# Attention on one core: the value product in two bursts a head, and two heads turned at once

## The chip, the cores and the metric

The kernel runs on one core of one Trainium2 chip. The metric is device time in microseconds (us). The program computes a small transformer in one launch: attention, a mixture of experts, a wavelet block with linear attention, and a second mixture of experts. The change touches the attention stage and a constant that it used.

## The reference

`x` has 4 sequences of 1024 tokens and 256 features; there are 16 heads of 16 features, so 64 (sequence, head) pairs. All is float32.

```python
Q, K, V = (proj(Wq, bq), proj(Wk, bk), proj(Wv, bv))
scale = 1.0 / jnp.sqrt(jnp.float32(hd))
scores = jnp.einsum('bhqd,bhkd->bhqk', Q, K) * scale
attn = jax.nn.softmax(scores, axis=-1)
out = jnp.einsum('bhqk,bhkd->bhqd', attn, V)
```

## The kernel before, in words

`stage_attention` works through the 64 heads, four to a loop iteration (`SLOTS`), first and last iteration written out (`peeled_ends`). Each engine has its own program and they meet at semaphores. For head n, with the 1024 keys in eight tiles `kt` of 128:

- TensorE (PE) makes transposed scores of a key tile, 128 keys by 1024 queries, as two products of 512 columns into `p_s[kt % 2]` (L507). ScalarE (ACT) takes the exponential into `pt` in SBUF (L541).
- Two heads ahead, PE makes the scores a second time, queries on partitions, in units of 128 by 512 (`max_unit`, L432), and VectorE (DVE) reduces each to a row maximum (L555). There are two units, `max0` and `max1`, for every `kt`. POOL negates the maxima and splits them into bf16 parts, PE turns them into rows (`rows_unit`, L440), DVE copies those (L569), and they enter the scores as two extra rows of the stack.
- These units go through `ring`, three PSUM banks. `claim(at)` makes PE wait until `ring_used` has reached `at - 2`, that is, until DVE has used unit `at - 3` and all before it.
- The value product `pv` (L454) multiplies `pt` by the padded values (16 features, a column of ones for the sum, zeros up to 32). Its result has only 32 rows, so four products run beside one another in the four column groups of the array: group `j = 2*qh + kh` takes query half `qh` and the even or odd key tile of the pair `2*i`, `2*i + 1`. One head has four such bursts of four calls, i = 0, 1, 2 after the scores of `kt` 3, 5, 7 and i = 3 after `kt` 1 of the next head. Each fp32 call shows as two records in the trace.
- ACT copies the accumulated `p_o`, 128 by 512, into `o_sb` (L530) after the exponential of `kt` 1 of the next head. `fold_unit` (L464) then multiplies each 128-column block by `c.fold`, which turns it (tokens onto partitions) and adds the halves for even and odd key tiles. The result goes into a ring bank, and DVE normalises from it (L577 reciprocal, L579 multiply).

The order of units in a head is written out in `units`: `max0`, scores, `rows` at `kt` 2, `max1`, burst, `fold` at `kt` 4. All engines derive the ring numbers from that list.

Of the kernel before, what the change touches and what calls it, by code (L numbers as in the profile page):

```python
# [8 lines left out]
ALU = mybir.AluOpType  # L9
# [89 lines left out]
def stage_constants(nc, mem, c):  # L99
# [3 lines left out]
    c.fold = mem.sb("fold", [P, 2 * 32])  # L103
    zeroed, made = mem.sem("consts_zeroed"), mem.sem("consts_made")
    with nc.Block() as block:
        @block.gpsimd
        def _(pool):
            nc.gpsimd.memset(c.ident[:, :], 0.0).then_inc(zeroed, 1)
            nc.gpsimd.memset(c.identb[:, :], 0.0).then_inc(zeroed, 1)
            nc.gpsimd.memset(c.fold[:, :], 0.0).then_inc(zeroed, 1)  # L110

            pool.wait_ge(zeroed, 3)
# [3 lines left out]

            fold = c.fold[:, :].rearrange("p (q r) -> p q r", q=2)
# [147 lines left out]
def stage_attention(nc, a, c, w1, w1_loaded):  # L265
# [8 lines left out]
    with ExitStack() as stack:  # L274
# [5 lines left out]
        o_sb = mem.sb("o_transposed", [P, HALF])  # L280
# [5 lines left out]
        rec = mem.sb("o_reciprocal", [P, 2, 4])  # L286
# [18 lines left out]
        FOLD_AT, ROWS_AT = 4, 2  # L305

        def units(first, last, u):

            for kt in range(KT):
# [6 lines left out]
                if kt == FOLD_AT and not (first and u == 0):  # L316
                    yield kt, "fold"
# [10 lines left out]
        PER_GROUP = SLOTS * (2 * KT + 2)  # L328
        assert PER_GROUP % RING == 0 and GROUPS == w1.shape[1]

        def count_before(g, first, last, u):

            inside = sum(len(list(units(first, last, w))) for w in range(u))
            if first:
                return PROLOGUE + inside
            return g * PER_GROUP + (PROLOGUE - 1 + inside)

        def bank(g, first, last, u, j):
            base = PROLOGUE if first else PROLOGUE - 1
# [7 lines left out]
        with nc.Block() as block:  # L347
# [40 lines left out]
            def _(pool):  # L388
# [36 lines left out]
            def _(pe):  # L425
# [18 lines left out]
                def pv(n, u, i):  # L444

                    pe.wait_ge(exp_done, n * KT + 2 * i + 2)
# [32 lines left out]
                def body(g, first, last):  # L479
                    for u in range(SLOTS):  # L480
# [5 lines left out]
                        def emit(kt, kinds):  # L486
                            for j, (step, kind) in todo:
# [5 lines left out]
                                elif kind == "fold":  # L493
                                    fold_unit(n - 1, at, out)
# [24 lines left out]
                pv(NH - 1, SLOTS - 1, KT // 2 - 1)  # L519
                end = count_before(GROUPS - 1, False, True, SLOTS)  # L520
                fold_unit(NH - 1, end, bank(GROUPS - 1, False, True, SLOTS, 0))

            @block.scalar
            def _(act):
                def copy_o(n, units_before):

                    act.wait_ge(pv_done, (n + 1) * (KT // 2))

                    act.wait_ge(ring_ready, units_before)
                    nc.scalar.activation(o_sb[:, :], p_o[:, :], ACT.Copy).then_inc(o_copied, 1)  # L530

                def body(g, first, last):
                    for u in range(SLOTS):
                        n = g * SLOTS + u
                        for kt in range(KT):

                            act.wait_ge(scores_ready, n * KT + kt + 1)
                            if kt % 2 == 0:

                                wait_from(act, pv_done, (n - 1) * (KT // 2) + kt // 2 + 1)  # L540
                            nc.scalar.activation(pt[:, kt, :], p_s[kt % 2][:, :], ACT.Exp, scale=SCALE)\  # L541
                                .then_inc(exp_done, 1)
                            if kt == 1 and not (first and u == 0):
                                copy_o(n - 1, count_before(g, first, last, u))
# [1488 lines left out]
```

## Time and profile before

| | us |
|---|---|
| median of 3 runs | 2200.02 (2199.92 to 2202.66) |
| span of the profiled execution | 2200.1 |
| attention stage, first ring product to last multiply | 114.3 to 932.3 |
| of 225 to 900 us: PE / DVE / ACT / POOL busy | 675.0 / 592.0 / 462.7 / 49.1 |
| one reduction, 128x512 | 0.686 |
| one exponential, 128x1024 | 1.022 |
| copy of `p_o`, 128x512 | 0.597 |

The profiled execution's own time is the span, 0.1 us from the median. "Busy" is the union of the records of an engine. Matmul records overlap and their ends are modelled, so PE's work is better read from the distance between starts. A timeline row merges equal neighbours; "x3" are three instructions, and the duration is that of all of them. "PEld" rows are weight loads. "[0.35 <-PE ps_ring L432]" means that the engine had been idle for 0.35 us and that this product ended it.

### The profile page before, as it was taken

The numbers are of one execution on the slowest core, as the hardware profiler recorded it, in microseconds if no ns is written. First come the engines' busy times: TensorE is split into PE (matmuls) and PEld (weight loads), VectorE is DVE, ScalarE is ACT, GpSimd is POOL, SyncE is SP. The second block draws the span as 40 slices with busy tenths as digits, with TensorE's granted clock in tenths as the row PEclk, the third lists the DMA queues.
The fourth block names the chain that finished last, engine by engine and source line by source line (L and its number), as shares of the span: only waits on it lengthen the run. The fifth ranks groups of instructions, "written<-read, shape, count | busy, mean of one in ns | idle before, by whom it ended". The sixth has DMA issues, their size and how long they took to land. (4 is left out here: it accounts for less than half of the span.)

```text
span 2200.1 us, 36075 instructions
## 1 busy us (share of the span) xinstructions
PE 1873.4 (85%) x9396; PEld 1027.7 (47%) x9397; DVE 1405.8 (64%) x3053; ACT 890.4 (40%) x1235; POOL 420.3 (19%) x561
## 2 busy tenths in 40 slices
PE   7899999999999999985699999999994885057771
PEld 4423333333333333363467766666673565036550
DVE  4588888888888888552744444444444897936335
ACT  3336666666666666732022222222221520021330
POOL 2210000000000000030023333333331001102771
PEclk9979999999999999987799999999997998575995
DMA  4511111111111111056111111221212000061224
GB/s 141 182 43 40 42 45 45 46 39 42 42 38 46 39 42 45 28 180 242 64 29 31 32 33 30 33 33 30 33 31 81 1 1 6 19 224 48 47 39 153
DMA packets 98995, 130.04 MB, mean 59 GB/s; under 512 B 19392, under 2 KB 78080, under 8 KB 98304
## 3 DMA queue, kind: packets, MB, share of 16 engines
q1 hardware_dynamic: 66400, 85.79, 12.4%
q0 software_dynamic: 21504, 23.72, 6.5%
q10 hardware_dynamic: 11040, 19.92, 2.6%
q8 instruction: 24, 0.39, 0.1%
q14 instruction: 27, 0.22, 0.0%
HBM read 94.93 MB, written 48.23 MB: 65 GB/s over the span
## 5 line engine op out<-in xcount | busy, mean ns | idle before, releaser
L555 DVE TENSOR_REDUCE unit_max<-ps_ring 128x1 f32<-128x512 f32 x1024 | 655.6, 686 | 85.1 <-PE ps_ring L432 74.8
L541 ACT ACTIVATE w<-ps_scores 128x1024 f32<-128x1024 f32 x512 | 509.8, 1022 | 268.2 <-PE ps_scores L507 256.4
L432 PE MATMUL ps_ring<-k_stack,q_stack 96*128 96x512 bf16 x1024 | 372.2, 392 | 9.8 <-POOL v_padded L395 9.2
L1272 PE MATMUL m_ps_y<-w,m_ht 128*128 (+1 forms) x1312 | 305.3, 382 | 32.3 <-DVE m_ht L1358 32.3
L507 PE MATMUL ps_scores<-q_stack,k_stack 98*128 98x512 bf16 x1024 | 306.6, 381 | 0.1
L1250 PE MATMUL m_ps_h<-w,m_xt 128*128 (+1 forms) x736 | 305.4, 554 | 1.2 <-ACT m_xt L1305 1.0
L454 PE MATMUL ps_o<-w,v_padded 128*32 128x512 f32 x2048 | 273.3, 606 | 0.6 <-ACT w L541 0.6
L1272 PEld LDWEIGHTS m_ps_y<-w,m_ht 128*128 128x128 f32 x1312 | 241.0, 190 | 68.5 <-DVE m_y L1366 33.4
L432 PEld LDWEIGHTS ps_ring<-k_stack,q_stack 96*128 96x128 bf16 x1024 | 102.2, 100 | 317.7 <-DVE unit_max L555 232.3
L1186 POOL DMA_INDIRECT sums<-m_y,m_is x112 | 177.8, 1588 | 266.7 <-ACT m_y L1298 244.7
L1365 DVE COPY m_is<-scatter 128x1 int32 (+1 forms) x112 | 17.3, 154 | 293.5 <-PE m_ps_y L1272 222.1
L1315 ACT ACTIVATE m_h<-m_h 128x512 f32<-128x512 f32 (+1 forms) x184 | 107.3, 583 | 238.2 <-DVE m_h L1348 237.1
L1250 PEld LDWEIGHTS m_ps_h<-w,m_xt 128*128 128x128 f32 x736 | 133.3, 193 | 109.5 <-issue 105.7
L1348 DVE TENSOR_TENSOR m_h<-m_ps_h,biases 128x512 f32<-128x512 f32 x144 | 99.7, 692 | 121.9 <-PE m_ps_h L1250 121.9
L1298 ACT ACTIVATE m_y<-m_y,gains 128x256 f32<-128x256 f32 x112 | 56.9, 508 | 280.0 <-DVE m_y L1366 280.0
L1178 POOL DMA_INDIRECT m_x<-rows,m_ig x112 | 110.5, 986 | 278.0 <-DVE m_ig L1341 251.6
L403 POOL TENSOR_SCALAR neg_max<-row_max 128x8 f32<-128x8 f32 x64 | 14.8, 232 | 709.2 <-DVE row_max L563 709.2
L507 PEld LDWEIGHTS ps_scores<-q_stack,k_stack 98*128 98x128 bf16 x1024 | 99.9, 99 | 80.3 <-issue 5.3
L1358 DVE COPY m_ht<-m_ps_t 128x512 f32<-128x512 f32 (+1 forms) x184 | 109.6, 628 | 9.3 <-PE m_ps_t L1263 1.9
L1263 PE MATMUL m_ps_t<-ident,m_h 128*128 128x128 f32 x656 | 91.0, 274 | 1.4 <-ACT m_h L1315 1.4
L454 PEld LDWEIGHTS ps_o<-w,v_padded 128*32 128x32 f32 x2048 | 40.4, 108 | 107.6 <-issue 85.0
L883 PE MATMUL g_ps_t<-ident,g_rows 128*128 128x128 f32 x128 | 22.8, 309 | 76.8 <-DMA g_w<-in_gate 76.8
(217 smaller groups left out, 1919.4 us busy)
## 6 DMA issues: line engine op xcount, KB each, us to landing
w<-in_w SPq DMA_DIRECT2D x16, 512.0 KB, 3.5
rows<-g_rows SPq DMA_DIRECT2D x16, 512.0 KB, 3.0
y<-sums SPq DMA_DIRECT2D x16, 512.0 KB, 6.8
q_parts<-qk_part SPq DMA_DIRECT2D x16, 384.0 KB, 3.3
k_parts<-qk_part SPq DMA_DIRECT2D x16, 384.0 KB, 3.8
q_stack<-q_parts SPq DMA_DIRECT2D x64, 96.0 KB
k_stack<-k_parts SPq DMA_DIRECT2D x64, 96.0 KB
xt<-in_xt ACTq DMA_DIRECT2D x8, 512.0 KB, 4.2
```

The costliest lines, as they stand in the source:

```text
L432: nc.tensor.matmul(out[:, :], qs[0:STACK, u, qt * P:(qt + 1) * P], ks[0:STACK, u, half * HALF:(half + 1) * HALF], start=True, stop=True).t ...
L454: mm = nc.tensor.matmul(p_o[32 * j:32 * j + 32, :], vpad[u % 2][:, 2 * i + kh, :], pt[:, 2 * i + kh, qh * HALF:(qh + 1) * HALF], start=(i ...
L507: mm = nc.tensor.matmul(p_s[kt % 2][:, half * HALF:(half + 1) * HALF], ks[:, u, kt * P:(kt + 1) * P], qs[:, u, half * HALF:(half + 1) * HALF],
L541: nc.scalar.activation(pt[:, kt, :], p_s[kt % 2][:, :], ACT.Exp, scale=SCALE)\
L555: nc.vector.tensor_reduce(unit_max[:, u % 2, half, qt:qt + 1], src[:, :], axis=AX.X, op=ALU.max).then_inc(ring_used, 1)
L1178: pool.indirect_dma_start(out=xg[u][:, :], out_offset=None, in_=rows, in_offset=bass.IndirectOffsetOnAxis(ap=ig[u][:, :], axis=0))\
L1186: pool.indirect_dma_start(out=sums, out_offset=bass.IndirectOffsetOnAxis(ap=isc[u][:, :], axis=0), in_=ys[u][:, :], in_offset=None, bounds ...
L1250: mm = nc.tensor.matmul(p_hs[u % BUFS][:, half * HW:(half + 1) * HW], xt[u][:, k, :], w1[:, bass.ds(e * KC + k, 1), half * HW:(half + 1) * HW]
L1272: mm = nc.tensor.matmul(p_y[:, 0:D], ht[u][:, f, :], w2[:, bass.ds(e * FC + f, 1), :].rearrange("p a d -> p (a d)"), start=(f == 0), stop= ...
L1315: nc.scalar.activation(span, span, func).then_inc(act_done, 1)
L1348: nc.vector.tensor_tensor(hs[u][:, half * HW:(half + 1) * HW], p_hs[u % BUFS][:, half * HW:(half + 1) * HW], b1[:, bass.ds(e, 1), half * H ...
L1358: nc.vector.tensor_copy(ht[u][:, :, :].rearrange("p f n -> p (f n)")[:, half * HW:(half + 1) * HW], p_t[:, half * HW:(half + 1) * HW]).the ...
```

## The change

- **Value product.** Group j takes query set j (128 queries of each half of the 1024, 256 columns in all) over all keys. A burst covers four key tiles, sixteen calls of 256 columns; a head has two bursts, i = 0 after `kt` 5 and i = 1 after `kt` 1 of the next head. `p_o` is used to column 256 and needs no adding of halves.
- **Turning.** `o_sb` holds two heads. In every second head (`u` even), after `kt` 3, four fp32 transposes with the identity turn both heads into one whole ring bank. The unit takes two ring numbers, `spare` and `fold`; the claim is for the second, so `ring_used` must reach `at - 1` for the spare's number `at`: the unit two before the spare has to be used.
- **Normalising.** One reciprocal of 16 columns and one multiply of 256 for two heads, with an increment of `ring_used` between.
- **Waits.** ACT waits for the value product at `kt` 0 and 4 instead of at every even `kt`. `c.fold` and what made it on POOL are gone.

```diff
@@ -100,26 +100,17 @@
-    c.fold = mem.sb("fold", [P, 2 * 32])
...
-            nc.gpsimd.memset(c.fold[:, :], 0.0).then_inc(zeroed, 1)
-
-            pool.wait_ge(zeroed, 3)
+
+            pool.wait_ge(zeroed, 2)
...
-            for kh in range(2):
-
-                pool.wait_ge(made, 2 + kh)
-                nc.gpsimd.affine_select(out=fold, in_=fold, compare_op=ALU.not_equal, fill=1.0, base=-32 * kh,
-                                        pattern=[[-64, 2], [-1, 32]], channel_multiplier=1).then_inc(made, 1)
...
-        FOLD_AT, ROWS_AT = 4, 2
+        FOLD_AT, ROWS_AT = 3, 2
+        BURST = KT // 2
...
-                if kt == FOLD_AT and not (first and u == 0):
+                if kt == FOLD_AT and u % 2 == 0 and not (first and u == 0):
+                    yield kt, "spare"
                     yield kt, "fold"
...
-                        wait_apart(pool, spare_p, pv_done, (n - 1) * 4)
+                        wait_apart(pool, spare_p, pv_done, (n - 1) * 2)
...
-                    pe.wait_ge(exp_done, n * KT + 2 * i + 2)
+                    pe.wait_ge(exp_done, n * KT + BURST * (i + 1))
...
-                    for kh in range(2):
-                        for qh in range(2):
-                            j = 2 * qh + kh
-                            mm = nc.tensor.matmul(p_o[32 * j:32 * j + 32, :], vpad[u % 2][:, 2 * i + kh, :],
-                                                  pt[:, 2 * i + kh, qh * HALF:(qh + 1) * HALF],
-                                                  start=(i == 0), stop=(i == KT // 2 - 1))
+                    for kt in range(BURST * i, BURST * (i + 1)):
+                        probs = pt[:, kt, :].rearrange("p (b j q) -> p j b q", b=2, j=4)
+                        for j in range(4):
+                            mm = nc.tensor.matmul(p_o[32 * j:32 * j + 32, 0:2 * P], vpad[u % 2][:, kt, :],
+                                                  probs[:, j, :, :], start=(kt == 0), stop=(kt == KT - 1))
...
-                    pe.wait_ge(o_copied, n + 1)
-                    claim(at)
+                    pe.wait_ge(o_copied, n + 2)
+                    claim(at + 1)
                     for blk in range(4):
-                        mm = nc.tensor.matmul(out[:, blk * 64:(blk + 1) * 64], o_sb[:, blk * P:(blk + 1) * P],
-                                              c.fold[:, :], start=True, stop=True)
-                    mm.then_inc(ring_ready, 1)
+                        mm = nc.tensor.transpose(out[:, blk * P:(blk + 1) * P],
+                                                 o_sb[:, blk // 2, blk % 2 * P:(blk % 2 + 1) * P], c.ident[:, :])
+                        if blk >= 2:
+                            mm.then_inc(ring_ready, 1)
...
-                                pv(n - 1, u + 1, KT // 2 - 1)
-                            if kt in (3, 5, 7):
-                                pv(n, u, (kt - 3) // 2)
+                                pv(n - 1, u + 1, 1)
+                            if kt == BURST + 1:
+                                pv(n, u, 0)
...
-                    nc.scalar.activation(o_sb[:, :], p_o[:, :], ACT.Copy).then_inc(o_copied, 1)
+                    nc.scalar.activation(o_sb[:, u % 2, :], p_o[:, 0:2 * P], ACT.Copy).then_inc(o_copied, 1)
...
-                            if kt % 2 == 0:
-
-                                wait_from(act, pv_done, (n - 1) * (KT // 2) + kt // 2 + 1)
+                            if kt % BURST == 0:
+
+                                wait_from(act, pv_done, (n - 1) * 2 + kt // BURST + 1)
...
-                def normalise(n, at, src):
-                    dve.wait_ge(ring_ready, at + 1)
+                def normalise(n, pair, at, src):
+                    dve.wait_ge(ring_ready, at + 2)
...
-                    o = src[:, 0:256].rearrange("p (b q r) -> p q b r", b=4, q=2)
-                    nc.vector.reciprocal(rec[:, :, :], o[:, :, :, HD]).then_inc(rec_done, 1)
-                    dve.wait_ge(rec_done, n + 1)
+                    o = src[:, :].rearrange("p (m r) -> p m r", r=32)
+                    nc.vector.reciprocal(rec[:, :], o[:, :, HD]).then_inc(rec_done, 1)
+                    dve.wait_ge(rec_done, pair + 1)
+                    nc.vector.sem_inc(ring_used, 1)
                     nc.vector.tensor_tensor(
...
```

PE's order around the turning, from the rows transpose of a head (`kt` 2) to the first unit of `kt` 4 or 5; `ps_ring` is the ring, `ps_scores` is `p_s`, `ps_o` is `p_o`, `w` is `pt`. Before:

```order
L507 MATMUL ps_scores<-q_stack,k_stack 128x512 x2
L440 MATMUL ps_ring<-identb,neg_parts 16x128
L432 MATMUL ps_ring<-k_stack,q_stack 128x512 x2
L507 MATMUL ps_scores<-q_stack,k_stack 128x512 x2
L432 MATMUL ps_ring<-k_stack,q_stack 128x512
L454 MATMUL ps_o<-w,v_padded 32x512 x4
L432 MATMUL ps_ring<-k_stack,q_stack 128x512
L507 MATMUL ps_scores<-q_stack,k_stack 128x512 x2
L432 MATMUL ps_ring<-k_stack,q_stack 128x512
L464 MATMUL ps_ring<-fold,o_transposed 128x64 x4
L432 MATMUL ps_ring<-k_stack,q_stack 128x512
```

After, from the unit ahead of the burst of `kt` 1 in such a head:

```order
L425 MATMUL ps_ring<-k_stack,q_stack 128x512
L447 MATMUL ps_o<-w,v_padded 32x256 x16
L425 MATMUL ps_ring<-k_stack,q_stack 128x512
L502 MATMUL ps_scores<-q_stack,k_stack 128x512 x2
L433 MATMUL ps_ring<-identb,neg_parts 16x128
L425 MATMUL ps_ring<-k_stack,q_stack 128x512 x2
L502 MATMUL ps_scores<-q_stack,k_stack 128x512 x2
L425 MATMUL ps_ring<-k_stack,q_stack 128x512
L456 MATMUL ps_ring<-ident,o_transposed 128x128 x4
L425 MATMUL ps_ring<-k_stack,q_stack 128x512
```

The burst of four at `kt` 3 and the fold of `kt` 4 are gone; one burst of sixteen calls stands at `kt` 1, and the four transposes stand between the two last units of `kt` 3 and the first of `kt` 4. Further on in the same head the order after the change is

```order
L502 MATMUL ps_scores<-q_stack,k_stack 128x512 x2
L425 MATMUL ps_ring<-k_stack,q_stack 128x512 x2
L502 MATMUL ps_scores<-q_stack,k_stack 128x512 x2
L425 MATMUL ps_ring<-k_stack,q_stack 128x512
L447 MATMUL ps_o<-w,v_padded 32x256 x16
L425 MATMUL ps_ring<-k_stack,q_stack 128x512
L502 MATMUL ps_scores<-q_stack,k_stack 128x512 x2
```

so that eight units of maxima stand between one burst and the next, where before there were four.

DVE's order at the normalisation, `unit_max` being the row maxima and `biases` the tile that holds the attention output. Before:

```order
L555 TENSOR_REDUCE unit_max<-ps_ring 128x1
L573 REGISTER_ALU
L577 RECIPROCAL o_reciprocal<-ps_ring 128x8
L579 ISA
L579 TENSOR_TENSOR biases<-ps_ring,o_reciprocal 128x128
L554 REGISTER_ALU
L555 TENSOR_REDUCE unit_max<-ps_ring 128x1
```

After:

```order
L550 TENSOR_REDUCE unit_max<-ps_ring 128x1
L568 REGISTER_ALU
L572 RECIPROCAL o_reciprocal<-ps_ring 128x16
L573 REGISTER_ALU
L575 ISA
L575 TENSOR_TENSOR biases<-ps_ring,o_reciprocal 128x256
L549 REGISTER_ALU
L550 TENSOR_REDUCE unit_max<-ps_ring 128x1
L549 REGISTER_ALU
```

The two instructions stand two reductions earlier in a head than before, in every second head only, each twice as wide, with an increment of `ring_used` (L573) between them.

## Rows read from the trace of the kernel before

**Rows 1.** The page: busy time and share; groups with busy us, mean ns, idle before.

```profile
PE 1873.4 (85%) x9396; PEld 1027.7 (47%) x9397; DVE 1405.8 (64%) x3053; ACT 890.4 (40%) x1235; POOL 420.3 (19%) x561
...
L454 PEld LDWEIGHTS ps_o<-w,v_padded 128*32 128x32 f32 x2048 | 40.4, 108 | 107.6 <-issue 85.0
```

**Rows 2.** Windows: busy us and count of each engine, PE clock, DMA share, GB/s.

```profile
115.00:125.00 10.00, 9.92 (x18) 1.67 (x16) 9.96 (x18) 0.00 (x0) 0.00 (x0) 0.50 0.20 60
225.00:900.00 675.00, 675.00 (x3946) 238.26 (x3946) 591.99 (x1081) 462.69 (x487) 49.08 (x216) 1.00 0.15 42
```

**Rows 3.** Timeline of a head: start, duration, engine, line, [idle before <- releaser].

```profile
601.33 0.69 DVE L555 TENSOR_REDUCE unit_max<-ps_ring 128x1 f32<-128x512 f32 x1 [0.30 <-PE ps_ring L432]
...
602.08 0.10 PEld L432 LDWEIGHTS ps_ring<-k_stack,q_stack 96*128 96x128 bf16 x1 [0.17 <-DVE unit_max L555]
...
602.24 1.89 DVE L555 TENSOR_REDUCE unit_max<-ps_ring 128x1 f32<-128x512 f32 x3
...
602.74 0.38 PE L432 MATMUL ps_ring<-k_stack,q_stack 96*128 96x512 bf16 x1
...
603.05 1.06 PE L454 MATMUL ps_o<-w,v_padded 128*32 128x512 f32 x8
...
604.05 0.39 PE L432 MATMUL ps_ring<-k_stack,q_stack 96*128 96x512 bf16 x1
...
604.48 1.34 DVE L555 TENSOR_REDUCE unit_max<-ps_ring 128x1 f32<-128x512 f32 x2 [0.35 <-PE ps_ring L432]
...
604.71 0.38 PE L432 MATMUL ps_ring<-k_stack,q_stack 96*128 96x512 bf16 x1
...
604.93 1.00 PE L464 MATMUL ps_ring<-fold,o_transposed 128*128 128x64 f32 x8
...
605.77 0.38 PE L432 MATMUL ps_ring<-k_stack,q_stack 96*128 96x512 bf16 x1
...
605.97 0.21 DVE L577 RECIPROCAL o_reciprocal<-ps_ring 128x8 f32<-128x8 f32 x1
...
606.53 1.28 DVE L555 TENSOR_REDUCE unit_max<-ps_ring 128x1 f32<-128x512 f32 x2
```

**Rows 4.** Timeline, the next head's fold.

```profile
617.43 0.33 PE L464 MATMUL ps_ring<-fold,o_transposed 128*128 128x64 f32 x2
```

**Rows 5.** Timeline, inside one burst: its weight loads; its second four records.

```profile
603.05 0.16 PEld L454 LDWEIGHTS ps_o<-w,v_padded 128*32 128x32 f32 x8 [0.42 <-ACT w L541]
...
603.51 0.61 PE L454 MATMUL ps_o<-w,v_padded 128*32 128x512 f32 x4
```

**Rows 6.** Timeline of the expert stage: 256-column products, then fp32 transposes.

```profile
1403.86 3.62 PE L1272 MATMUL m_ps_y<-w,m_ht 128*128 x16
1407.32 1.04 PE L1263 MATMUL m_ps_t<-ident,m_h 128*128 128x128 f32 x8
1408.19 1.02 PE L1250 MATMUL m_ps_h<-w,m_xt 128*128 x2
```

**Rows 7.** Timeline of DVE around the combination of a head's maxima.

```profile
608.16 2.54 DVE L555 TENSOR_REDUCE unit_max<-ps_ring 128x1 f32<-128x512 f32 x4 [0.35 <-PE ps_ring L432]
610.73 0.17 DVE L563 TENSOR_TENSOR row_max<-unit_max 128x8 f32<-128x8 f32 x1
610.99 0.69 DVE L555 TENSOR_REDUCE unit_max<-ps_ring 128x1 f32<-128x512 f32 x1
```

**Rows 8.** Timeline, the last head's fold and its reciprocal.

```profile
930.96 1.10 PE L464 MATMUL ps_ring<-fold,o_transposed 128*128 128x64 f32 x8 [0.72 <-ACT o_transposed L530]
932.11 0.21 DVE L577 RECIPROCAL o_reciprocal<-ps_ring 128x8 f32<-128x8 f32 x1 [6.35 <-PE ps_ring L464]
```

**Rows 9.** Timeline of POOL's constants and the first load.

```profile
1.75 0.28 POOL L114 TENSOR_SCALAR_AFFINE_SELECT identb<-identb 128x128 bf16<-128x128 bf16 x1
2.18 0.63 POOL L121 TENSOR_SCALAR_AFFINE_SELECT fold<-fold 128x64 f32<-128x64 f32 x2
...
3.12 0.45 SPq L150 DMA_DIRECT2D w_qkv<-in_wqkv  x1
```

More of the change, by code:

```diff
@@ L279, in stage_attention @@
         vpad = [mem.sb(f"v_padded{u}", [P, KT, 32]) for u in range(2)]
-        o_sb = mem.sb("o_transposed", [P, HALF])
+        o_sb = mem.sb("o_transposed", [P, 2, 2 * P])
         unit_max = mem.sb("unit_max", [P, 2, 2, KT])
@@ L285, in stage_attention @@
         negt = [mem.sb(f"neg_rows{u}", [MAXROWS * KT, P], BF16) for u in range(2)]
-        rec = mem.sb("o_reciprocal", [P, 2, 4])
+        rec = mem.sb("o_reciprocal", [P, 2 * KT])
         p_s = [mem.ps(f"ps_scores{u}", (P, S)) for u in range(2)]
@@ L327, in first_units @@
                 yield (at, None, 0, 0) if at == FIRST_ROWS else (at, n // (2 * KT), n % (2 * KT) // 2, n % 2)
-        PER_GROUP = SLOTS * (2 * KT + 2)
+        PER_GROUP = SLOTS * (2 * KT + 1) + 2 * (SLOTS // 2)
         assert PER_GROUP % RING == 0 and GROUPS == w1.shape[1]
@@ L335, in count_before @@
                 return PROLOGUE + inside
-            return g * PER_GROUP + (PROLOGUE - 1 + inside)
+            return g * PER_GROUP + (PROLOGUE - 2 + inside)
         def bank(g, first, last, u, j):
-            base = PROLOGUE if first else PROLOGUE - 1
+            base = PROLOGUE if first else PROLOGUE - 2
             return ring[(base + sum(len(list(units(first, last, w))) for w in range(u)) + j) % RING]
@@ L493, in emit @@
                                 elif kind == "fold":
-                                    fold_unit(n - 1, at, out)
+                                    fold_unit(n - 2, at - 1, out)
+                                elif kind == "spare":
+                                    continue
                                 else:
@@ L513, in body, with copy_o @@
                             if kt == 1 and not (first and u == 0):
-                                pv(n - 1, u + 1, KT // 2 - 1)
-                            if kt in (3, 5, 7):
-                                pv(n, u, (kt - 3) // 2)
+                                pv(n - 1, u + 1, 1)
+                            if kt == BURST + 1:
+                                pv(n, u, 0)
                             emit(kt, ("fold",))
                 groups(pe, body)
-                pv(NH - 1, SLOTS - 1, KT // 2 - 1)
+                pv(NH - 1, SLOTS - 1, 1)
                 end = count_before(GROUPS - 1, False, True, SLOTS)
-                fold_unit(NH - 1, end, bank(GROUPS - 1, False, True, SLOTS, 0))
+                fold_unit(NH - 2, end, bank(GROUPS - 1, False, True, SLOTS, 1))
             @block.scalar
             def _(act):
-                def copy_o(n, units_before):
-                    act.wait_ge(pv_done, (n + 1) * (KT // 2))
+                def copy_o(n, u, units_before):
+                    act.wait_ge(pv_done, (n + 1) * 2)
                     act.wait_ge(ring_ready, units_before)
-                    nc.scalar.activation(o_sb[:, :], p_o[:, :], ACT.Copy).then_inc(o_copied, 1)
+                    nc.scalar.activation(o_sb[:, u % 2, :], p_o[:, 0:2 * P], ACT.Copy).then_inc(o_copied, 1)
                 def body(g, first, last):
@@ L543, in body @@
                             if kt == 1 and not (first and u == 0):
-                                copy_o(n - 1, count_before(g, first, last, u))
+                                copy_o(n - 1, u + 1, count_before(g, first, last, u))
                 groups(act, body)
-                copy_o(NH - 1, count_before(GROUPS - 1, False, True, SLOTS))
+                copy_o(NH - 1, SLOTS - 1, count_before(GROUPS - 1, False, True, SLOTS))
             @block.vector
@@ L600, in body @@
                             elif kind == "fold":
-                                normalise(n - 1, at, src)
+                                normalise(n - 2, g * 2 + (u // 2 - 1), at - 1, src)
+                            elif kind == "spare":
+                                continue
                             else:
@@ L607, in _ @@
                 end = count_before(GROUPS - 1, False, True, SLOTS)
-                normalise(NH - 1, end, bank(GROUPS - 1, False, True, SLOTS, 0))
+                normalise(NH - 2, NH // 2 - 1, end, bank(GROUPS - 1, False, True, SLOTS, 1))
         mem.clear()
```

5 lines of the change are left out of this document (2 added, 3 removed).

## Prediction

> **What bounds the kernel now.** I read the page first: TensorE (PE) is busy 85% of the span [rows 1]. The change touches the attention stage, so next I read that stage alone: from 225 to 900 us PE is busy all the time at the full granted clock (2.4 GHz), VectorE (DVE) 88%, ScalarE (ACT) 69% [rows 2]. Then the timeline of one head. The period is exact: the fold starts at 604.93 and again at 617.43 [rows 3, 4], so a head takes 12.50 us and two take 25.00. PE's starts follow each other without a wait that matters: it is the bound, by the length of what it executes. But DVE is close behind, and what ties the two is the ring of three PSUM banks: PE may write a ring unit only when DVE has used the unit three before it.
>
> From rows 3 I take these pieces (us):
> - PE: one 512-column bf16 product every 0.22; ring product to next ring product with two scores between, 0.66 (604.05 to 604.71). Last product to burst, 0.31 (602.74 to 603.05), 0.09 more than 0.22. Burst to next product, 1.00. Fold, 0.84 (604.93 to 605.77).
> - PE to DVE: product start to its reduction's start, 0.43 (604.05 to 604.48).
> - DVE: first two reductions after a burst, 0.65 apart (1.34 - 0.69); 0.91 where the rows transpose comes between (601.33 to 602.24); 0.60 apart when they queue (1.89 - 0.68, halved).
> - DVE to PE: reduction start to the product that had waited for that bank, 0.75 (601.33 to 602.08, named as the wait).
>
> **Part 1, the bursts.** Four bursts of 4 calls become two of 16 calls with half the columns; each call is two matmul records. Four column groups run together: four records start at 603.05 and the other four at 603.51, while their eight weight loads, of 108 ns each [rows 1], all fall into 0.16 us, so they are issued within 0.05 [rows 5]. A record at full width takes 0.216 us for 256 columns (16 in 3.46 us, 1403.86 to 1407.32) [rows 6]. A new burst is eight waves of four records. The old burst takes 0.14 us more than its two waves of 0.43: the exposed first weight load and the step back to full width. I keep that once per burst: 8 x 0.216 + 0.14 = 1.87. Unseen is whether short waves join without a seam. Lower end: no exposed load, 0.025 less, 1.85. Upper end: if the 0.025 that the second wave came late (0.455 against 0.43) recurs on every seam, 7 x 0.025 more, 2.04. I take 1.87, since that lateness is explained by the first load alone. For PE alone two old bursts cost 2 x (0.09 + 1.00) = 2.18 and one new one 0.09 + 1.87 = 1.96: it saves 0.22, twice a head, 0.88 a pair.
>
> Eight loads issued within 0.05 us show that issue would not limit a wave, which needs eight instructions in 0.216. A rule that would speak against it is in the Trainium skill, TensorE: Matmul & The Clock Gate, section "Wait — 56ns, not 53.3ns?": without hardware decoding the sequencer spends about 62 ns on a matmul. By that estimate the 32 of a burst need 1.98 us instead of 1.73, 0.25 x 4 x 30.5 = 31 us more than the sum below. The trace speaks against it.
>
> **Part 2, the fold.** Per pair two folds of 0.84 go; one group of four fp32 transposes comes: eight records in 0.87 us (1407.32 to 1408.19) [rows 6], no drain on either side there. PE saves 0.80 a pair.
>
> **Part 3, DVE.** Per pair one normalisation instead of two. Today its reciprocal to the next reduction is 0.56 (605.97 to 606.53) [rows 3]. With 256 results instead of 128 the multiply grows by about 0.13 (a 512-element reduction takes 0.69, so some 1 ns an element, an estimate) and the reciprocal by 0.01: 0.70. DVE saves 0.42 a pair.
>
> **Part 4, the ring.** This decides. During a burst PE makes no ring units, and with three banks DVE holds at most three reductions, 1.8 us of work. From the last product before a burst to the first reduction after it passes 0.31 + 1.00 + 0.43 = 1.74 us today, and DVE idles 0.35 (its row at 604.48 [rows 3]); with the new burst it is 2.61, and DVE idles nearly 1 us. It loses 1.9 us a head in two pauses where it lost 1.4 in four. Today's idle costs nothing, PE being the bound. The new one can't be made good, for between bursts PE would run ahead (two units and two scores take it 0.87, DVE 1.20), and the ring holds it to DVE's pace. So I walk half a head, time 0 at the first product after a burst, eight units to the next burst:
> - Half with the rows transpose: reductions of units 1 to 4 start at 0.43, 1.34, 1.94, 2.54. Unit 7 is written at 2.54 + 0.75 = 3.29, unit 8 0.66 later, 3.95.
> - Half with the maxima's combination after unit 4: unit 5's reduction at 0.43 + 0.65 + 3 x 0.60 = 2.89, plus the combination. That is 0.31 (between 0.28, if only its 0.17 and 0.71 latency count, and 0.37, as from 610.02 to 610.99) [rows 7]: 3.20. Unit 8 is written at 3.95.
> Each half then ends with 0.31 + 1.87: 6.13 us, 12.26 a head without a fold, against a PE sum of some 11.65.
> - The transposes, in every second head, must find the bank two back free: unit 3's reduction (1.94) + 0.75 = 2.69. Stalled at its first load the fold needs 1.15 to the reciprocal (930.96 to 932.11) [rows 8], 0.03 more for the wider ones: 3.87. Unit 5's reduction comes at 3.87 + 0.70 = 4.57; unit 7 waits for the multiply's end, about 3.87 + 0.85 = 4.72, and unit 8 is written at 5.38, 1.43 later than without.
> Sum for a pair: 4 x 6.13 + 1.43 = 25.95 against 25.00, 0.95 more. ACT, 69% busy, has room, and its copy is halved. POOL's value copy and SP's loads wait for events that still come microseconds early, so I cost those waits at nothing.
>
> **Ends.** The constant work that goes from POOL is, in the main, what stands between 2.03 and 2.81, ahead of the first DMA at 3.12 [rows 9]: -0.8. At the end the last burst lies bare (1.00 to 1.87), less some 0.2 for a copy of half the width (an estimate), plus 0.14 for the multiply and 0.03 for the transposes, and the last two heads, paced by ACT, meet longer bursts: +2, between 0 and 3.
>
> **Sum.** Heads 1 to 61 have both halves, 30.5 pairs: 30.5 x 0.95 = 29.0. With +2 and -0.8 that makes 30; the terms are rounded upwards by about 0.02 a half, so I take 29. The profiled span, 2200.1, is the runs' median, 2200.0, within 0.1. Forecast 2229 us.
>
> DVE's wait of 0.35 us after each burst [rows 3] is the first sign of this limit. The Trainium skill (TensorEngine Tiling (Array Packing), section "PSUM Bottleneck") warns that column tiling speeds up the array and not the emptying of PSUM, which may become the bound. The trace does not show that yet, PE being the bound; the walk says that the change brings it about.
>
> **Rivals.**
> - A. PE stays the bound: the pair costs 25.00 - 0.88 - 0.80 = 23.32, 30.5 x -1.68 = -51, and 2150 us. For it: PE is busy without a gap, DVE only 88%. Against it: it needs DVE to work 10.7 of 11.65 us a head with two pauses near 1 us. It decides only if the pause were under 0.4. 7%.
> - B. The walk is right but waves have seams or are issued late: 7 x 0.025 x 4 x 30.5 = +21, 2250. 12%.
> - C. The pieces of the walk overlap more than I add them: the bank back after 0.65, the first reduction after 0.38, the transposes stalled 0.3 less. That is (0.10 + 0.05) x 4 + 0.3 = 0.9 a pair and takes the whole cost away: 2202; half of it gives 2215. The 0.75 and the 0.43 are read directly, which speaks against it. 10%, a quarter of that within 0.2% of before.
> - D. The waits, up to 0.6 us, cost PE its clock. From 115 to 125 us, with the ring alone running, the granted clock was 0.50, which is 1.2 GHz [rows 2]. Low for a tenth of the stage, it adds a tenth of 11.65 a head, 61 x 1.2 = 71 more: 2300. Against it: PE's pauses stay near a tenth of a half head. The Trainium skill (TensorE: Matmul & The Clock Gate, section "A second HAM failure mode: psum-queue depth-cycling") describes such an oscillation where PE pauses between groups of products; it would have this price. 3%.
> The walk itself: 68%, its own range 2215 to 2243.
>
> **Numbers.** Under 2206 lie A and part of C, above 2258 D and part of B: range 2206 to 2258. A measurement here tells about 0.2% (4.4 us) from no change. Faster 0.08 (A and a little), same 0.03, slower 0.89.
>
> **What would show it.** Burst to next product 1.87; DVE waiting 0.9 to 1.0 us for PE after each of two bursts a head; PE's ring products waiting for DVE up to 0.6, most ahead of the transposes; reciprocal to reciprocal 25.9 us. A spacing near 23.3 would prove A, bursts over 2.0 us B, a clock under 1.00 from 225 to 900 us D.

## The result and the profile after

| | before | after |
|---|---|---|
| median (lowest to highest), us | 2200.57 (2199.92 to 2202.66), 4 runs | 2228.43 (2227.46 to 2230.03), 4 runs |
| span of the profiled execution | 2200.1 | 2227.4 |
| two heads, in the steady part | 25.00 | 25.78 |
| last reciprocal of the attention | 932.11 | 953.81 |

The changed kernel is slower: 1.0121 times the time of before, with a 95% interval of 1.0107 to 1.0135. The forecast was 2229.

Engines first, from the page of the kernel after. It answers to [rows 1]; the columns of a group are busy us and mean ns, then the idle time ahead and its releaser:

```profile
PE 1855.9 (83%) x11060; PEld 1065.3 (48%) x11061; DVE 1383.5 (62%) x2989; ACT 880.4 (40%) x1235; POOL 420.0 (19%) x558
...
L550 DVE TENSOR_REDUCE unit_max<-ps_ring 128x1 f32<-128x512 f32 x1024 | 641.5, 684 | 133.3 <-PE ps_ring L425 126.1
```

The steady part of the attention in the windows view of the kernel after (columns as in [rows 2]):

```profile
225.00:900.00 675.00, 639.51 (x5180) 260.58 (x5173) 555.79 (x996) 440.88 (x472) 47.41 (x208) 1.00 0.15 41
```

PE was busy all 675 us before [rows 2]; now 35 us are gaps. DVE is less busy too (556 against 592). Two engines that both become idler while neither has got more to do wait for each other. The clock is not the reason: 1.00, 2.4 GHz, in both. Who waits for whom, 225 to 900 us; columns: total us, times, longest. First after:

```profile
PEld ps_ring L425 <- DVE unit_max L550: 177.4, 474, 1.0
...
DVE unit_max L550 <- PE ps_ring L425: 100.9, 118, 0.9
...
PEld ps_ring L456 <- DVE unit_max L550: 24.9, 26, 1.0
...
PE ps_ring L425 <- DVE unit_max L550: 17.6, 82, 0.5
...
PE ps_ring L456 <- DVE unit_max L550: 12.1, 26, 0.5
```

and before:

```profile
PEld ps_ring L432 <- DVE unit_max L555: 193.2, 281, 0.8
...
DVE unit_max L555 <- PE ps_ring L432: 56.2, 164, 0.5
```

DVE pauses less often (118 times against 164) but for 0.9 us instead of 0.3, and PE has waits for DVE that it did not have before. A PEld wait by itself costs nothing, since a weight load may wait beneath the product that runs; the two PE rows are real gaps. They understate the loss: a product's record lasts 0.39 us, but the next can start 0.22 after it, so a product that starts 0.17 late shows no gap. The starts tell more. Take each step from one product to the next in run 4 below, where none is held up, and count what the same step takes longer: over 20 pairs of heads PE is held up by 0.10 us a pair before and by 2.87 after. What is left, 24.90 and 22.91, is the pair that PE's own work would need.

Now one head in the timeline of the kernel after, with the transposes, then the head's second half. It answers to [rows 3]:

```profile
624.94 0.39 PE L425 MATMUL ps_ring<-k_stack,q_stack 96*128 96x512 bf16 x1
...
625.37 0.69 DVE L550 TENSOR_REDUCE unit_max<-ps_ring 128x1 f32<-128x512 f32 x1 [0.88 <-PE ps_ring L425]
...
626.28 1.89 DVE L550 TENSOR_REDUCE unit_max<-ps_ring 128x1 f32<-128x512 f32 x3
...
627.62 0.66 PE L456 MATMUL ps_ring<-ident,o_transposed 128*128 128x128 f32 x4 [0.46 <-DVE unit_max L550]
...
628.22 0.39 PE L425 MATMUL ps_ring<-k_stack,q_stack 96*128 96x512 bf16 x1
...
628.31 0.26 DVE L572 RECIPROCAL o_reciprocal<-ps_ring 128x16 f32<-128x16 f32 x1
...
628.82 0.43 DVE L575 TENSOR_TENSOR biases<-ps_ring,o_reciprocal 128x256 f32 x1 [0.24 <-DVE o_reciprocal L572]
...
629.16 2.47 DVE L550 TENSOR_REDUCE unit_max<-ps_ring 128x1 f32<-128x512 f32 x4
...
630.27 1.93 PE L447 MATMUL ps_o<-w,v_padded 128*32 128x256 f32 x32
...
632.14 0.39 PE L425 MATMUL ps_ring<-k_stack,q_stack 96*128 96x512 bf16 x1
...
632.56 2.54 DVE L550 TENSOR_REDUCE unit_max<-ps_ring 128x1 f32<-128x512 f32 x4 [0.93 <-PE ps_ring L425]
...
636.39 1.93 PE L447 MATMUL ps_o<-w,v_padded 128*32 128x256 f32 x32
...
638.26 0.39 PE L425 MATMUL ps_ring<-k_stack,q_stack 96*128 96x512 bf16 x1
```

Now the starts. The burst, 630.27, to the next product, 632.14: 1.87 us. DVE's reductions of the ring run dry during it: it had been idle for 0.93 us at 632.56. The half head without transposes lasts from 632.14 to 638.26, 6.12 us. The half with them lasts 7.20 (624.94 to 632.14), and in it PE stood still 0.46 us until DVE had freed the bank for the transposes. In [rows 3] DVE was idle 0.35 after a burst and PE not at all.

### The profile page after: what moved, and what is told of

Same layout as the page of the kernel before. It is cut to its first block and busy times, and to the rows that moved or that the text cites. A ratio compares the mean times of both kernels' runs of the same rounds, so it can differ in the third digit from the quotient of the medians.

```text
span 2227.4 us, 39134 instructions
## 1 busy us (share of the span) xinstructions
PE 1855.9 (83%) x11060; PEld 1065.3 (48%) x11061; DVE 1383.5 (62%) x2989; ACT 880.4 (40%) x1235; POOL 420.0 (19%) x558
## 5 line engine op out<-in xcount | busy, mean ns | idle before, releaser
L550 DVE TENSOR_REDUCE unit_max<-ps_ring 128x1 f32<-128x512 f32 x1024 | 641.5, 684 | 133.3 <-PE ps_ring L425 126.1
L447 PE MATMUL ps_o<-w,v_padded 128*32 128x256 f32 x4096 | 247.6, 382 | 1.6 <-ACT w L536 1.6
L447 PEld LDWEIGHTS ps_o<-w,v_padded 128*32 128x32 f32 x4096 | 120.0, 109 | 100.9 <-issue 19.4
```

What stands on the lines that cost most here:

```text
L447: mm = nc.tensor.matmul(p_o[32 * j:32 * j + 32, 0:2 * P], vpad[u % 2][:, kt, :], probs[:, j, :, :], start=(kt == 0), stop=(kt == KT - 1))
L550: nc.vector.tensor_reduce(unit_max[:, u % 2, half, qt:qt + 1], src[:, :], axis=AX.X, op=ALU.max).then_inc(ring_used, 1)
```

## The experiments

The theory: the saving on PE is real, but three banks hold too little work to carry DVE over a burst of 1.87 us; its lost time can't be made good, and the ring hands it on to PE. The rivals: the new shape of the products or the transposes are themselves the cost, or the place of the transposes and their claim on two ring units. "Pair" is the distance between reciprocals over two heads in the profiled execution; ratios are against the kernel before in the same job.

| run | what it is | median us | ratio (95%) | pair us |
|---|---|---|---|---|
| 1 | after, four bursts of 2 key tiles | 2176.24 | 0.988 (0.9864 to 0.9897) | 24.17 |
| 2 | before, two bursts of 4 key tiles | 2253.50 | 1.0239 (1.0222 to 1.0256) | 26.52 |
| 3 | after, reductions read 256 columns | 2146.71 | 0.9754 (0.9738 to 0.977) | 23.42 |
| 4 | before, reductions read 256 columns | 2190.04 | 0.9945 (0.9929 to 0.9962) | 24.88 |
| 5 | after, three bursts, transposes at `kt` 7 | 2168.03 | 0.9838 (0.9822 to 0.9854) | 23.95 |
| 6 | after, three bursts, transposes at `kt` 3 | 2182.23 | 0.9907 (0.9891 to 0.9923) | 24.33 |
| 7 | after, transposes at `kt` 7 | 2224.63 | 1.0098 (1.0081 to 1.0114) | 25.58 |
| 8 | after, unchanged | 2227.18 | 1.0116 (1.0097 to 1.0135) | 25.78 |
| 9 | before, unchanged | 2202.05 | 0.9998 (0.9988 to 1.0007) | 25.00 |
| 10 | after, reductions read 384 columns | 2170.16 | 0.9853 (0.9836 to 0.987) | 24.04 |

### 1. The new groups and transposes, with four bursts

Against the kernel after:

```diff
-        BURST = KT // 2
+        WIDTHS = (2, 2, 2, 2)
+        STARTS = tuple(sum(WIDTHS[:i]) for i in range(len(WIDTHS)))
+        BURSTS = len(WIDTHS)
...
-                    for kt in range(BURST * i, BURST * (i + 1)):
+                    for kt in range(STARTS[i], STARTS[i] + WIDTHS[i]):
...
-                                pv(n - 1, u + 1, 1)
-                            if kt == BURST + 1:
-                                pv(n, u, 0)
+                                pv(n - 1, u + 1, BURSTS - 1)
+                            if kt in (3, 5, 7):
+                                pv(n, u, (3, 5, 7).index(kt))
```

> The changed kernel with the query-set groups and the paired transposes kept, but four bursts a head of two key tiles each (after kt 3, 5, 7 and 1 of the next head) as before. Theory (ring): a burst is as long as before, 1.00 us, DVE idles about 0.4 us after each, four units lie between bursts and the ring holds no one back; PE is the bound again and keeps what the transposes save. The walk gives 24.1 us a pair against 25.00 before and 25.8 after: about 2200 - 0.95 x 30.5 = 2171 us, between 2165 and 2180. Rival (the query-set groups cost in themselves, by twice as many loads and records): no better than 2200.

Measured: 2176.24 (2172.68 to 2178.07), 1.2% faster than before, pair 24.17. Its timeline and its window from 225 to 825 us:

```profile
609.42 1.07 PE L449 MATMUL ps_o<-w,v_padded 128*32 128x256 f32 x16
...
610.42 0.39 PE L427 MATMUL ps_ring<-k_stack,q_stack 96*128 96x512 bf16 x1
...
610.85 0.69 DVE L552 TENSOR_REDUCE unit_max<-ps_ring 128x1 f32<-128x512 f32 x1 [0.30 <-PE ps_ring L427]
```

```profile
225.00:825.00 600.00, 595.93 (x4922) 235.80 (x4920) 532.81 (x943) 412.44 (x447) 44.58 (x196) 1.00 0.16 44
```

The burst is 1.00 us again, DVE's pause 0.30, PE is busy 99%. So neither the query-set groups nor the paired transposes are the cost: with short bursts they gain 0.83 us a pair. By the starts PE's own work is 23.75, 1.15 less than before, and 0.42 is given back, most of it at the third ring product after the transposes, which starts some 0.3 late because DVE is at the wide multiply. What follows for the cause: it lies in the length of the burst.

### 2. The long bursts alone

Against the kernel before; groups, calls and fold stay:

```diff
-                    for kh in range(2):
+                    for kt in range(4 * i, 4 * i + 4):
                         for qh in range(2):
-                            j = 2 * qh + kh
-                            mm = nc.tensor.matmul(p_o[32 * j:32 * j + 32, :], vpad[u % 2][:, 2 * i + kh, :],
-                                                  pt[:, 2 * i + kh, qh * HALF:(qh + 1) * HALF],
-                                                  start=(i == 0), stop=(i == KT // 2 - 1))
+                            j = 2 * qh + kt % 2
+                            mm = nc.tensor.matmul(p_o[32 * j:32 * j + 32, :], vpad[u % 2][:, kt, :],
+                                                  pt[:, kt, qh * HALF:(qh + 1) * HALF],
+                                                  start=(kt < 2), stop=(kt >= KT - 2))
...
-                            if kt in (3, 5, 7):
-                                pv(n, u, (kt - 3) // 2)
+                            if kt == 5:
+                                pv(n, u, 0)
```

> The kernel before with only the bursts merged: two bursts a head of four key tiles, 512-column calls, old groups, old folding product of every head at kt 4. Theory (ring): the same burst length as the changed kernel, 1.87 us, the same two pauses of DVE, and two normalisations a pair: the walk gives 26.1 us a pair, 1.1 over before, and 0.2 more at the loop's end: 2234 to 2245 us. Rival (the loss of the change comes from the transposes and the two ring numbers they hold): below 2200, since two steps between tiling modes are saved.

Measured: 2253.50 (2252.52 to 2255.18), 2.4% slower than before. The one edit costs 53 us and takes the kernel past the changed one. Its timeline:

```profile
606.63 1.92 PE L454 MATMUL ps_o<-w,v_padded 128*32 128x512 f32 x16
...
608.49 0.39 PE L432 MATMUL ps_ring<-k_stack,q_stack 96*128 96x512 bf16 x1
...
608.91 2.54 DVE L555 TENSOR_REDUCE unit_max<-ps_ring 128x1 f32<-128x512 f32 x4 [1.11 <-PE ps_ring L432]
```

The burst takes 1.86 and DVE's pause is 1.11. The time lies 8.5 us above the range expected. The spacing of reciprocals: three of four heads take 13.15, and every fourth, which holds the end of the loop (below), 13.59. The expectation had the loop's end, 0.2 a pair, and it is there (0.22). What it had too low is the walk's pair without it, 26.1 against 26.30. A head has one half of 6.11 us, as walked, and one of 7.04 with the fold, where 6.92 was left. In all the pair is 0.22 over the 26.3 expected, 6.7 us in 30.5 pairs.

### 3 and 4. A cheaper reduction, in both kernels

The maximum is taken over 256 of each unit's 512 columns, so half of the keys do not enter it. The same edit in both:

```diff
-                    nc.vector.tensor_reduce(unit_max[:, u % 2, half, qt:qt + 1], src[:, :], axis=AX.X,
+                    nc.vector.tensor_reduce(unit_max[:, u % 2, half, qt:qt + 1], src[:, 0:HALF // 2], axis=AX.X,
```

> The changed kernel with each reduction to the row maximum reading 256 of the unit's 512 columns (it leaves out half of the keys in the maxima). The products, bursts and transposes stay. Theory (ring): DVE is no longer the slow side, about 0.36 a unit, so PE runs unheld and its own sum shows, 23.7 us a pair: 2150 to 2165 us, over 60 below the changed kernel. Rival (long bursts or the smaller calls cost PE time of their own): stays within 10 us of 2228.

> The kernel before with the same halved reductions (it leaves out half of the keys in the maxima). Theory (ring): PE is the bound already, so next to nothing: 2193 to 2201 us. Rival (DVE bounds the kernel before as well): tens of us faster, as in the changed kernel.

Measured: the changed kernel falls to 2146.71 (2145.74 to 2149.63), the kernel before only to 2190.04 (2188.01 to 2192.54). The changed kernel with the cheap reduction, timeline and window:

```profile
611.81 1.93 PE L447 MATMUL ps_o<-w,v_padded 128*32 128x256 f32 x32
...
613.68 0.39 PE L425 MATMUL ps_ring<-k_stack,q_stack 96*128 96x512 bf16 x1
...
614.10 0.42 DVE L550 TENSOR_REDUCE unit_max<-ps_ring 128x1 f32<-128x256 f32 x1 [1.76 <-PE ps_ring L425]
```

```profile
225.00:825.00 600.00, 596.78 (x5086) 247.53 (x5087) 352.51 (x973) 417.92 (x461) 46.30 (x204) 1.00 0.16 45
```

DVE now pauses 1.76 us after a burst, longer than ever, and it costs next to nothing, since PE is the bound: a pause is only harmful where DVE lacks the time to make it good. The pair from the reciprocals:

```profile
598.67 0.26 DVE L572 RECIPROCAL o_reciprocal<-ps_ring 128x16 f32<-128x16 f32 x1 [0.21 <-PE ps_ring L456]
...
621.99 0.26 DVE L572 RECIPROCAL o_reciprocal<-ps_ring 128x16 f32<-128x16 f32 x1 [0.21 <-PE ps_ring L456]
...
645.51 0.26 DVE L572 RECIPROCAL o_reciprocal<-ps_ring 128x16 f32<-128x16 f32 x1 [0.21 <-PE ps_ring L456]
```

23.32 and 23.52 alternate, 23.42 in the mean, 0.3 under the 23.7 expected. Even here PE is held up by 0.56 a pair, at the transposes (0.19) and at a few ring products; 22.86 is its own work. Against 24.88, before with the same reduction and nothing held up, that is 2.02 less. Rival A had 1.68 for PE's saving (0.88 + 0.80); the difference is in the transposes, as told below.

Both times lie some 3 us under the range expected, for a reason that I had left out: ahead of the first head there are only ring units, and there DVE is the bound (9.96 of 10 us busy [rows 2]). The first value product starts at 132.4 instead of 141.3 in the one and at 131.8 instead of 140.8 in the other. In part that is the clock: with the cheap reduction the granted clock is already 0.98 and 1.00 from 120 to 125 us, where both kernels with the full one still have 0.50. In the steady part the kernel before moves by 0.12 a pair, the kernel after by 2.36.

### 5 and 6. Three bursts

Against the kernel after; as in run 1, with

```diff
-        FOLD_AT, ROWS_AT = 3, 2
-        BURST = KT // 2
+        FOLD_AT, ROWS_AT = 7, 2
+        WIDTHS = (3, 3, 2)
+        STARTS = tuple(sum(WIDTHS[:i]) for i in range(len(WIDTHS)))
+        BURSTS = len(WIDTHS)
...
+                            if kt in (4, 7):
+                                pv(n, u, (4, 7).index(kt))
```

Run 6 is the same with `FOLD_AT` left at 3.

> Three bursts a head of 3, 3 and 2 key tiles (after kt 4, 7 and 1 of the next head), query-set groups, and the transposes after the burst of kt 7 instead of at kt 3. Theory (ring): one more change of tiling mode saved against four bursts, DVE's pauses between those of four and of two bursts, and the transposes find their banks free. The walk gives 23.8 us a pair, and about 24.0 with what the walk has left out so far, against 24.17 with four bursts: 2165 to 2176 us. Rival (any burst longer than before loses by the ring): above 2180.

> The same three bursts with the transposes at kt 3, where DVE has a backlog and the claim for two ring numbers must wait. Theory (ring): 0.5 us a pair more than at kt 7, 24.5: 2180 to 2192 us. Rival (the place of the transposes is indifferent, PE being the bound): the same as at kt 7 within 4 us.

Measured: 2168.03 (2163.02 to 2169.02, 5 runs) with the transposes after `kt` 7, and 2182.23 (2181.45 to 2182.84) with them after `kt` 3. Both times are as expected; the pair of run 6 is 0.17 below its 24.5. The faster of the two, timeline and window:

```profile
609.63 1.50 PE L449 MATMUL ps_o<-w,v_padded 128*32 128x256 f32 x24
...
611.49 3.73 DVE L552 TENSOR_REDUCE unit_max<-ps_ring 128x1 f32<-128x512 f32 x6 [0.50 <-PE ps_ring L427]
```

```profile
225.00:825.00 600.00, 595.95 (x4957) 244.42 (x4955) 530.49 (x953) 412.09 (x452) 45.51 (x200) 1.00 0.16 45
```

A burst of 1.44 leaves a pause of 0.50, and PE stays 99% busy. By the starts, PE's own work in a pair is 22.9 with two bursts a head, 23.3 with three and 23.75 with four: each further burst adds its step in and out, 0.22 to 0.23 (0.14 + 0.09). Held up is 2.87 with two, 0.64 with three and 0.42 with four, so three bursts with the transposes after `kt` 7 have the shortest pair of the versions with full reductions. This version beats both kernels, 1.6% under the one before. Not all of its lead is the burst's: with the transposes left at `kt` 3, three bursts take 24.33, longer than four (24.17), and four bursts with the transposes after `kt` 7 were not run.

### 7. The transposes elsewhere

```diff
-        FOLD_AT, ROWS_AT = 3, 2
+        FOLD_AT, ROWS_AT = 7, 2
```

> The changed kernel with the transposes at kt 7 instead of kt 3. Theory (ring): both places lie in a stretch of eight units in which the ring holds PE to DVE, so only the stall of the transposes differs; the walk gives 0.14 us a pair less: 2220 to 2228 us. Rival (the wait for two ring numbers at kt 3 is the cause of the change's loss): some 0.8 us a pair less, under 2208.

Measured: 2224.63 (2222.48 to 2225.71), pair 25.58, 0.21 less than after. Of the 0.78 that the change costs a pair, 0.58 stays: the place of the transposes is not the cause. The claim on two ring numbers is still there in this run, and PE still waits 0.64 us for it (0.62 at `kt` 3); that the loss does not need it is shown by run 2, which has no such claim and loses more. The transposes with a claim on one number were not run. With three bursts the same move is worth 0.38 a pair (runs 5 and 6): there PE no longer waits at the transposes, and what it is held up falls from 1.02 to 0.64.

### 8 and 9. Both kernels once more, unchanged

They have no edit. They ask how much of the difference between two profiles is in code that was not changed.

> The changed kernel once more, unchanged. Its first profile spent 5.6 us more behind the attention stage than the profile before, in code that is the same in both; all profiles so far lie between 1266 and 1274 us there. Theory (the part behind the attention varies from execution to execution): somewhere in 1266 to 1274 again, with 25.78 us a pair in the attention as before. Rival (the change slows what comes behind): 1273 or more again.

> The kernel before once more, unchanged, for a second profile. Theory (variation): 12.50 us a head, and the part behind the attention anywhere in 1266 to 1274. Rival (the change slows what comes behind): 1268 or less again.

Measured: 2227.18 (2226.02 to 2229.66) and 2202.05 (2199.33 to 2205.06), the same pairs to 0.01 us. Behind the last reciprocal of the attention, where the code is the same, the two profiled executions of the kernel after take 1273.6 and 1271.1 us, those of the kernel before 1268.0 and 1269.4, and the other experiments between 1266.0 and 1276.5. That stretch varies by some 5 us either way with no clear order that follows the change.

### 10. Three quarters of the reduction

The maximum is taken over 384 of the 512 columns, so a quarter of the keys do not enter it.

```diff
-                    nc.vector.tensor_reduce(unit_max[:, u % 2, half, qt:qt + 1], src[:, :], axis=AX.X,
+                    nc.vector.tensor_reduce(unit_max[:, u % 2, half, qt:qt + 1], src[:, 0:3 * HALF // 4], axis=AX.X,
```

> The changed kernel with each reduction reading 384 of 512 columns (a quarter of the keys is left out of the maxima). Theory (ring): a reduction then takes about 0.47 instead of 0.60, which already brings DVE's pace near PE's, so nearly all of the gain of the halved one comes: 23.4 to 23.9 us a pair, 2160 to 2172 us. Rival (the time simply follows DVE's work, in proportion): half of the gain, 24.5 a pair, about 2188.

Measured: 2170.16 (2169.96 to 2173.06), pair 24.04 (23.84 and 24.25 alternate). Its window:

```profile
225.00:825.00 600.00, 585.17 (x4942) 244.82 (x4938) 429.97 (x949) 407.31 (x450) 45.49 (x199) 1.00 0.16 43
```

If the time simply followed DVE's work, three quarters would stand half way between 25.78 and 23.42, at 24.60. The first quarter gives 1.74 of the 2.36 us, the second 0.62: DVE's pace counts while it is the bound, and less and less once PE is. The pair came out 0.14 over what the walk said (23.4 to 23.9), the time inside its range.

## Why the prediction was right, and what was off in it

**The burst.** Predicted 1.87, measured 1.87 (630.27 to 632.14). Short waves join without a seam, and the sequencer does not slow them: 32 records in 1.73 us after the 0.14 is 54 ns each. The 62 ns that the Trainium skill gives for a matmul without hardware decoding (TensorE: Matmul & The Clock Gate, section "Wait — 56ns, not 53.3ns?") do not show here; whether these runs had hardware decoding, none of them tells. Rival B is out.

**The ring.** Half a head without the transposes: walked 6.13, measured 6.12. DVE's pause after each burst: predicted 0.9 to 1.0, measured 0.88 and 0.93. Runs 1 to 4 show that this is what makes the kernel slower: take the long burst away and the loss becomes a gain, bring it alone and the loss is there, make DVE faster and it goes. The Trainium skill warns that tiling speeds up the array but not the emptying of PSUM (TensorEngine Tiling (Array Packing), section "PSUM Bottleneck"). The traces agree only in that DVE's emptying of banks became the bound; the banks are those of the full-width ring products, and the value product ran in four column groups before as well. What moved is the length of the burst, with 0.35 us of pause before and 0.93 after. Rival A fell on its own condition: the pause is not under 0.4. Its pair for PE's own work, 23.32, was too long; the starts give 22.9.

**The transposes: a mis-sized term.** Part 2 took eight records for the four transposes and 0.87 us. The page of the kernel after counts them:

```profile
L456 PE MATMUL ps_ring<-ident,o_transposed 128*128 128x128 f32 x128 | 20.9, 286 | 14.6 <-DVE unit_max L550 14.1 <-ACT o_transposed L525 0.5
```

128 records in 32 pairs are four each, and [rows 6] had shown eight transposes, not four. So four take 0.44; from the first of them to the next product it is 0.49 where nothing is waited for (625.25 to 625.74 in run 1). PE saves 1.18 a pair with them, not 0.80. From the first one to the reciprocal it is 0.69 us (627.62 to 628.31), where Part 4 had 1.18. Against that, the normalisation is longer: reciprocal to next reduction 0.85 (628.31 to 629.16) instead of 0.70, since the 256-element multiply takes 0.43 and only starts 0.51 after the reciprocal. The half with transposes is 6.13 + 1.43 = 7.56 walked, less 0.49, plus 0.15: 7.22; measured 7.20.

**The end of the loop: a missed term.** Every fourth head one reduction starts late. After, around a loop's end:

```profile
647.38 0.17 DVE L558 TENSOR_TENSOR row_max<-unit_max 128x8 f32<-128x8 f32 x1
...
648.01 1.89 DVE L550 TENSOR_REDUCE unit_max<-ps_ring 128x1 f32<-128x512 f32 x3 [0.46 <-PE ps_ring L425]
...
648.75 0.39 PE L425 MATMUL ps_ring<-k_stack,q_stack 96*128 96x512 bf16 x1 [0.53 <-DVE unit_max L550]
```

The combination to the next reduction takes 0.63 here and 0.18 at 635.14 in other heads. The product that it reads, the fifth after the burst, had been started at 646.21, so the "PE" in the bracket is only the last semaphore event. DVE itself was on its way through the loop's branch and registers (the trace has these instructions on DVE from 647.40 to 647.96), which no row counts as busy. It costs 0.44, 0.22 a pair. The trace of before held the same step, which I had not looked for, having read heads without it [rows 7]:

```profile
635.72 0.17 DVE L563 TENSOR_TENSOR row_max<-unit_max 128x8 f32<-128x8 f32 x1
...
636.35 3.18 DVE L555 TENSOR_REDUCE unit_max<-ps_ring 128x1 f32<-128x512 f32 x5 [0.46 <-PE ps_ring L432]
```

It took 0.63 there too, 0.26 in other heads, and cost nothing, because PE was the bound: reciprocals stayed 12.50 apart.

Together: 4 x 6.12 + 1.08 (7.20 - 6.12) + 0.22 = 25.78, as measured. The steady term is 30.5 x 0.78 = 23.9, not 29.0. This term was too large by 5.

**The start.** Predicted -0.8. The first load shows it:

```profile
2.26 0.45 SPq L141 DMA_DIRECT2D w_qkv<-in_wqkv  x1
```

It was at 3.12 [rows 9], so -0.86; but the first ring product, at 114.31 before, is at 113.94, 0.37 earlier. In the second profiles it is 0.20 (113.84 and 113.64), and over all runs that product starts anywhere from 112.4 to 114.7, so no more can be said than that the 0.86 does not show there.

**The clock in the first heads: chance.** The attention starts at half clock, 1.2 GHz. Two windows of the kernel before, of the kernel after, and of the kernel before once more (run 9):

```profile
135.00:140.00 5.00, 5.00 (x13) 1.55 (x12) 4.02 (x8) 3.07 (x3) 0.84 (x4) 0.50 0.00 0
140.00:145.00 5.00, 5.00 (x26) 1.05 (x24) 3.45 (x6) 2.88 (x3) 0.00 (x0) 0.81 0.00 1
```

```profile
135.00:140.00 5.00, 5.00 (x18) 1.57 (x15) 4.43 (x9) 3.70 (x5) 0.62 (x3) 0.74 0.00 1
140.00:145.00 5.00, 4.85 (x45) 1.94 (x44) 4.07 (x8) 3.02 (x5) 0.00 (x0) 1.00 0.01 3
```

```profile
135.00:140.00 5.00, 5.00 (x21) 1.41 (x19) 4.47 (x8) 3.62 (x4) 0.53 (x3) 0.76 0.00 1
140.00:145.00 5.00, 5.00 (x32) 1.71 (x32) 4.40 (x8) 3.23 (x4) 0.00 (x0) 1.00 0.01 3
```

By these means the granted clock rose at about 141.9 before and at 137.6 after, 4.3 us earlier. But in run 9, the same kernel as before, it rose at 137.4, in run 8 at 136.4, and in run 7, the changed kernel with the transposes elsewhere, only at 144.5. So when it rises differs from execution to execution, and the lead is mostly luck of the first profile. From the first ring product to the 65th the kernel before took 46.14 us and in run 9 44.34; the kernel after took 43.25 and 42.97. The lead of 2.9 in the first comparison is 1.4 in the second. The kernel after gives it back at 0.78 a pair (+0.7 at ring product 256, +7.0 at 512, +13.2 at 768, +20.0 at the last).

**The end of the attention.** Predicted +2. The last ring product is 20.0 later, the last reciprocal 21.7: +1.7. It answers to [rows 8]:

```profile
953.12 0.66 PE L456 MATMUL ps_ring<-ident,o_transposed 128*128 128x128 f32 x4 [0.50 <-ACT o_transposed L525]
953.81 0.26 DVE L572 RECIPROCAL o_reciprocal<-ps_ring 128x16 f32<-128x16 f32 x1 [18.28 <-PE ps_ring L456]
```

**The sum.** 23.9 - 0.4 - 2.9 + 1.7 = 22.3 by terms, 21.7 by the reciprocals; the 0.6 between them stays open. The profiles differ by 27.3: the other 5.6 lie behind the attention, 1268.0 against 1273.6, in unchanged code that varies by as much over the runs. The medians differ by 27.9 in the first comparison and by 23.3 in run 8's; the profiles of runs 8 and 9 differ by 25.0, 23.3 of it up to the last reciprocal. So the forecast of +29 is right in sign and mechanism, and its last few microseconds are luck: a steady term 5 too large was made good by a stretch behind the attention that took longer in that comparison. Whether the change moves the code behind it by a microsecond or two can't be told from these runs.

Rival C (pieces overlapping more than added) is out as well: the transposes came 0.49 sooner, but by the wrong count and not by an overlap, and the bank's return (0.74, 648.01 to 648.75) and the way from product to reduction (0.42, 632.14 to 632.56) did not shrink. Rival D is out, at a clock of 1.00.

## What to carry to other kernels

A burst on one engine must fit into what the ring ahead of it buffers: compare the gap that the consumer sees (last unit before the burst to the first after it) with the work it holds in the banks, and with the slack it has in a period to make a pause good. Where the consumer was 88% busy, going from four bursts to two saved 0.22 us of switching for each one that went, but made each pause 0.93 us instead of 0.35, and PE was held up by 2.9 us a pair instead of 0.4. The best version run had the length between (three bursts) and the transposes moved with it. A pair is read as the mean over a whole round of the loop, since it can alternate. And count what a trace row merges: records per call, and the head in which the loop turns round.

## What the runs showed of the hardware

- Four column groups of fp32 products with 256 columns each follow in waves of 0.216 us without a seam; a burst costs 0.14 us on its own and 0.09 at the last product ahead, whether it has 16, 24 or 32 records.
- An fp32 transpose of 128 by 128 is one record and takes 0.109 us when others of its kind run ahead, while an fp32 product shows as two records of 0.216 per 256 columns.
- When a product comes to be held up by less than the overlap of two records (0.17 us), no idle time shows; the distances between starts do show it.
- DVE's way through the end of a loop costs 0.44 us when DVE is the engine that counts; the profile shows it as idle time and names a releaser that was ready long before.
- A reduction of 512, 384 and 256 columns takes 0.684, 0.550 and 0.421 us: 0.16 us is fixed, 1.03 ns an element.
